# State's output behind the whole down projection, two PSUM banks exchanged, one addition of VectorE moved forward

## The chip, the cores and the metric

One core of a Trainium2 chip. The core has five engines that run side by side and wait for each other through semaphores: TensorE (PE: matmuls, reads SBUF, writes PSUM), VectorE (DVE), ScalarE (ACT), GpSimd (POOL, no access to PSUM) and SyncE (SP, which only issues transfers here). PSUM has eight banks of 128 x 512 fp32. The metric is the device time of one execution in microseconds; the median of the runs is given.

## What is computed

The input `x` has 8 sequences of 1024 tokens with 256 features. One block of a network, in fp32:

```
n  = layernorm(x)
xp, z = split(n @ w_in)                  # 512 features each
xc = silu(causal_conv(xp, 4 taps) + conv_b)
h_t = 0.9 * h_(t-1) + 0.1 * (xc_t @ w_B) # a state of 16 numbers, along the sequence
y  = (h @ w_C) * silu(z)
x  = x + y @ w_out
n  = layernorm(x)
idx = top2(n[:, token 0, :] @ Wr + br)   # two of eight experts for the whole sequence
x  = x + mean over idx of (gelu(n @ W1[e] + b1[e]) @ W2[e] + b2[e])
```

`h @ w_C` is "state's output", `xc @ w_B` "state's input", the last matmul the "down projection".

## The kernel before

**Tiles.** The 8192 tokens are cut into 16 chunks of 512 (two for a sequence; `NC` = 16, `LAST` = 15). Activations stand with features on the partitions and the 512 tokens along the free axis, so a block of 128 features is one PSUM bank. The 512 inner features are four blocks (`JD`), the hidden features of the two chosen experts four more (`JF`). Each fp32 operand is split into a high part (fp32r) and a low rest, and a product is three matmuls: high by high, high by low, low by high. Hence the many "hi" and "lo" tiles: ScalarE makes the high parts, VectorE or GpSimd the low ones.

**Steps.** The kernel is a software pipeline, written out by hand for each engine. Step s works on three chunks at once: the first half of the block on chunk a = s, the output projection of chunk o = s - 1, the experts of chunk f = s - 2. Steps 3 to 13 or so run through a loop that holds an even step (`q` = 0, in which the experts of a new sequence are chosen) and an odd one (`q` = 1); the first chunks are an opening of their own, and steps 15, 16 and 17 are written out.

**TensorE's order in a step** (`step`, L1571 to L1616), which is fixed: in an even step the six small score matmuls of the router; four blocks of the input projection (`xp`, 6 matmuls of 128x512 each) into banks blk0 to blk3; the output projection (`out_proj`, 48 matmuls of 128x256) into tok0 and tok1; four blocks of z; four blocks of the up projection (`up`), both into blk0 to blk3; state's input (`state_in`, 8 matmuls) into turn1; then the down projection (`down`, L1440), whose half 0 (tokens 0 to 255 of the chunk) goes to bank tok0 and half 1 to tok1, 24 matmuls of 128x256 a half, six for each hidden block. State's output (`state_out`, L1478, 4 matmuls of 128x512) stands in the middle of half 1: behind its hidden blocks 0 and 1 and in front of 2 and 3. Its four blocks go to blk0 to blk3, each behind the gelu that empties the bank. L1296, L1299 and L1305 are the three matmuls of `project`; L1419, L1420 and L1421 those of `tokens`, used by both the output and the down projection.

**What follows state's output.** VectorE multiplies each block by the gate (`ys`, L1048; semaphore `y_set` counts the blocks), ScalarE takes the high part (`y_his`, L737), GpSimd the low one (`split_y`, L485), and the output projection of the next step uses them. The bank of a block is free when the product is done, so block j of the next step's input projection waits for it (`xp`, L1324).

**VectorE's order at the end of a step** (L1146 to L1231): the low parts of the hidden blocks (`hidden_lo`), the scan over the 512 tokens (`scan`), `edge`, the low part of the state (`state_lo`), the low part of the next chunk's normalized block (`turn1_lo`), then the four products `ys`, then `finish(f, q, 0)` and `finish(f, q, 1)`. A `finish` (L1053) adds one half of the down projection (a PSUM bank tok) to the residual; it waits for `down_ready` of that half and for `b2_added`, GpSimd's addition of the bias (L498). Behind it stands the next step: in an even one the `route` (L1065, four tiny operations that read the score), then the convolution: three taps for each block on VectorE (L992), the first pair waiting for ScalarE's `first_taps` (L678), which reads the bank of the input projection.

**Banks.** turn1 holds state's input from chunk 2 on, read by the scan. turn0 holds the score of the middle pairs of chunks (`score_bank`, L249). In the last chunks both serve transposes.

**GpSimd's order in an even step** (L592 to L603): `split_y`, the reciprocal root and the norm of the next chunk (`pow1`, `norm1`), low parts of the chosen W1, two low parts of the convolution (`split_conv`), W2, the third, the statistics of the second norm, the fourth, the bias sum, the bias add. State's input waits for the low parts.

Of the kernel before, what the change touches and what calls it, by code (L numbers as in the profile page):

```python
# [22 lines left out]
def build_block(nc, x, w_in, conv_w, conv_b, w_B, w_C, w_out, Wr, br, W1, b1, W2, b2, out):  # L23
# [19 lines left out]
    with ExitStack() as ctx:  # L43
# [187 lines left out]
        def z_bank(a, j):  # L231
            if isinstance(a, int) and a < 3:
                return (tok[j % 2], spread_banks[j], (turn[1], tok[0], tok[1], tok[1])[j])[a]
            return blk[j]

        def c_bank(a, j):
            if isinstance(a, int) and a < 2:
                return (spread_banks[j], (blk[1], blk[2], tok[0], blk[3])[j])[a]
            return blk[j]

        def u_bank(a):
            if isinstance(a, int) and a < 2:
# [6 lines left out]
        def score_bank(pair):  # L249
            if isinstance(pair, int) and pair in (0, NC // 2 - 1):  # L250
                return blk[0] if pair else blk[1]
            return turn[0]

        def edges_before(c, pair):
            if isinstance(c, int) and c < 4:
# [15 lines left out]
        def has_attn(s):  # L271
            return not isinstance(s, int) or s <= LAST

        def has_next(s, ahead):
            return not isinstance(s, int) or s + ahead <= LAST
# [583 lines left out]
        def _(dve):  # L859
# [91 lines left out]
            def turn1_lo(c):  # L951
                for k in range(KD):
                    dve.wait_ge(t1_hi, c * KD + k + 1)
                    if on_pe(c):
                        lo(xn1(c)[1][:, k, :], turn[k][:], xn1(c)[0][:, k, :]).then_inc(t1_lo, 1)
                    else:
                        lo(in_order(xn1_lo, k), regrouped(normed1, k), in_order(xn1_hi, k)).then_inc(t1_lo, 1)
# [90 lines left out]
            def ys(a, js=range(JD)):  # L1048
                for j in js:
                    dve.wait_ge(c_ready, a * JD + j + 1)  # L1050
                    nc.vector.tensor_tensor(gate_of(a, j), c_bank(a, j)[:], gate_of(a, j), ALU.mult).then_inc(y_set, 1)

            def finish(f, q, h):  # L1053
                dve.wait_ge(down_ready, f * 2 + h + 1)
                dve.wait_ge(b2_added, f + 1)
                rows = mid(f, q)[:, half_rows(h), :].rearrange("p n d -> p (n d)")
                nc.vector.scalar_tensor_tensor(rows, tok[h][:], 1.0 / TOP_K, rows, ALU.mult, ALU.add).then_inc(done, 1)
# [88 lines left out]
            def step(s, q, half):  # L1146
                a, o, f = s, s - 1, s - 2
                halves = half - 1 if q == 0 else half
                if q == 0 and not has_attn(s):
                    last_split((1, 2, 3))  # L1150
                    route(half - 1)
                    finish(f - 1, 1, 1)
                    turn2_lo(f)
                    residual(o, 1, halves, 0)
                    residual(o, 1, halves, 1)
                    stats2(o, 1)
                    hidden_lo(f, range(JF))
                    norm2_last()
                    turn2_lo(o)
                    finish(f, 0, 0)  # L1160
                    finish(f, 0, 1)
                    return
                if q == 0:
                    route(half - 1)
                    if has_attn(s):
                        taps(a, 0)
                    turn_squares2(f)
                    if has_attn(s):
                        taps(a, 1)
                    residual(o, 1, halves, 0)  # L1170
                    residual(o, 1, halves, 1)
                    turn2_lo(f)
                    stats2(o, 1)
                    if has_next(s, 2):
                        stats1(a + 2)
                        moments1(a + 2)
                    if has_next(s, 1):
                        turn_squares(a + 1)
                    hidden_lo(f, range(JF))
                    if has_attn(s):  # L1180
                        scan(a, 0)
                    if has_next(s, 1):
                        edge(a + 1, False)
                    if has_attn(s):
                        state_lo(a, 0)
                    if has_next(s, 1):
                        turn1_lo(a + 1)
                    if has_attn(s):
                        ys(a)
                    finish(f, 0, 0)  # L1190
                    finish(f, 0, 1)
                    return
                if not has_attn(s):
                    hidden_lo(f, range(JF))
                    finish(f, 1, 0)
                    finish_tile(f, 1, 2, tok[1])
                    finish_tile(f, 1, 3, turn[0])
                    return
                taps(a, 0)
                if isinstance(a, int) and a == 3:  # L1200
                    taps(a, 1)
                    turn_squares2(f)
                    turn2_lo(f)
                else:
                    turn_squares2(f)
                    taps(a, 1)
                residual(o, 0, halves, 0)
                residual(o, 0, halves, 1)
                if not (isinstance(a, int) and a == 3):
                    turn2_lo(f)  # L1210
                stats2(o, 0)
                if has_next(s, 2):
                    stats1(a + 2)
                if has_next(s, 2):
                    moments1(a + 2)
                if has_next(s, 1):
                    turn_squares(a + 1)
                hidden_lo(f, range(JF))
                scan(a, 1)
                if has_next(s, 1):  # L1220
                    edge(a + 1, True)
                state_lo(a, 1)
                if has_next(s, 1):
                    turn1_lo(a + 1)
                if has_next(s, 1):
                    ys(a)
                    finish(f, 1, 0)
                    finish(f, 1, 1)
                else:
                    finish(f, 1, 0)  # L1230
                    ys(a)  # L1231

            opening()
            steps(dve, step)
# [2 lines left out]
        def _(pe):  # L1237
# [80 lines left out]
            def xp(a, j):  # L1318
                if isinstance(a, int) and a == 1:
                    pe.wait_ge(tap_added, last_tap(0, j))  # L1320
                elif isinstance(a, int) and a == 2:
                    pe.wait_ge(tap_added, last_tap(1, j))
                elif not (isinstance(a, int) and a == 0):
                    pe.wait_ge(y_set, a * JD - JD + j + 1)  # L1324
                in_proj(a, j, 0, blk[j], xp_ready)

            def xp_first():
# [243 lines left out]
            def step(s, q, half):  # L1571
                a, o, f = s, s - 1, s - 2
                if q == 0:
                    score(f, half - 1)
                if has_attn(s):
                    for j in range(JD):
                        xp(a, j)
                if has_out(s):
                    out_proj(o, 0, (x_tail, a + 1) if has_attn(s) else None)
                    out_proj(o, 1)  # L1580
                if has_attn(s):
                    z(a)
                if q == 0:
                    pe.wait_ge(route_step, half * 3 - 2)
                up(s, f, q, half - 1)
                if has_attn(s):
                    pe.wait_ge(t2_lo, f * KD + KD)
                    state_in(a)
                if q == 0 and has_attn(s):
                    pe.wait_ge(w2_lo_set, (half - 1) * TOP_K + TOP_K)  # L1590
                if has_out(s):
                    pe.wait_ge(mid_set, o * 2 + 2)
                else:
                    pe.wait_ge(done, f * 2 + 3)
                if not has_out(s):
                    down(f, 0, (0, 1, 2), (up_tail, 2))
                    pe.wait_ge(done, f * 2 + 4)
                    down_tile(f, 2, tok[1][:, 0:D], (0, 1, 2))
                    down(f, 0, (3,))
                    down_tile(f, 2, tok[1][:, 0:D], (3,))  # L1600
                    down_tile(f, 3, turn[0][:, 0:D])
                    return
                if isinstance(s, int) and s == NC:
                    down(f, 0, (0, 1, 2), (up_tail, 1))
                    down(f, 1, (0, 1))
                    down(f, 0, (3,))
                    turns2(o)
                    down(f, 1, (2, 3))
                    return
                down(f, 0, range(JF), (state_tail, a + 1))  # L1610
                down(f, 1, (0, 1))
                if has_attn(s):
                    state_out(a, s)
                if isinstance(s, int) and s == LAST:
                    turns2(LAST - 1)
                down(f, 1, (2, 3))  # L1616
# [27 lines left out]
```

## Time and profile before

| | us |
|---|---|
| median of 3 runs | 505.83 (505.81 to 506.48) |
| the profiled execution, whole | 507.02 |
| its span, from the first to the last instruction | 505.1 |
| busy: TensorE, VectorE, ScalarE, GpSimd | 500.6, 450.9, 401.3, 348.1 |

The time of an execution holds some two microseconds around the span. Busy time adds up the durations of an engine's instructions where they don't overlap. A matmul's recorded duration (about 0.39 us for 128x512, 0.28 for 128x256) is longer than the distance to the next one, because they are pipelined; how fast TensorE goes is read from the starts. A VectorE operation likewise may start a little before the recorded end of the one before.

### The profile page before, as it was taken

How to read it: one execution, taken by the hardware profiler on the slowest of the kernel's cores; microseconds unless marked ns; L12 is line 12 of the kernel's file. 1: busy time of each engine (PE TensorE's matmuls, PEld its weight loads, DVE VectorE, ACT ScalarE, POOL GpSimd, SP SyncE). 2: the span in 40 equal slices, each digit the busy share in tenths (PEclk: the TensorE clock that was granted, in tenths of full speed). 3: DMA queues.
4: the chain of work that ended last, by engine and by line, in shares of the span. 5: the costliest groups of instructions: out<-in, count | busy, mean ns of one | idle time of the engine just before them, and what ended most of it. 6: DMA issues, size and time to landing. Idle time of an engine off the chain costs nothing.

```text
span 505.1 us, 9943 instructions
## 1 busy us (share of the span) xinstructions
PE 500.6 (99%) x3026; PEld 442.7 (88%) x3026; DVE 450.9 (89%) x896; ACT 401.3 (79%) x692; POOL 348.1 (69%) x390
## 2 busy tenths in 40 slices
PE   8999999999999999999999999999999999999997
PEld 8888799888888988889888888988889889888997
DVE  6999999889998999989999899998999989996763
ACT  4986959888969788697987969878796888969454
POOL 4959597559693796929869197773977559673390
PEclk9999999999999999999999999999999999999999
DMA  8940105344250532605235170433614343130102
GB/s 254 300 180 7 37 1 183 110 135 160 77 191 27 166 125 86 204 30 193 68 126 165 48 227 16 166 125 100 191 42 150 99 132 120 59 108 1 42 3 84
DMA packets 53380, 57.29 MB, mean 113 GB/s; under 512 B 8682, under 2 KB 49642, under 8 KB 53226
## 3 DMA queue, kind: packets, MB, share of 16 engines
q1 hardware_dynamic: 51498, 56.67, 34.5%
q10 hardware_dynamic: 1856, 0.31, 0.3%
q8 instruction: 13, 0.21, 0.2%
q14 instruction: 13, 0.11, 0.1%
HBM read 35.46 MB, written 21.50 MB: 113 GB/s over the span
## 4 chain that ended last, share of the span: by engine, by line
PE 98%; DVE 1%; DMA 1%; issue 0%; DVEq 0%
PE blk L1296 16%; PE blk L1299 16%; PE blk L1305 16%; PE tok L1419 12%; PE tok L1420 12%; PE tok L1421 12%; PE blk L1494 3%; PE turn L1470 3%; PE turn L1473 3%; PE turn L1243 1%; PE tok L1299 1%; PE tok L1296 1%; PE tok L1305 1%; DMA x_mid<-in_L_attn_x 1%; DVE stats_t L917 0%; DVE normed L934 0%
## 5 line engine op out<-in xcount | busy, mean ns | idle before, releaser
L992 DVE SCALAR_TENSOR_TENSOR conv<-blk,tap_w,conv 128x512 f32<-128x512 f32 x192 | 130.1, 741 | 8.2 <-ACT conv L683 7.1
L488 POOL TENSOR_TENSOR y_lo<-gate,y_hi 128x512 fp32r<-128x512 f32 x57 | 72.2, 1297 | 35.5 <-ACT y_hi L611 35.4
L1296 PE MATMUL blk<-xn_hi,w_in_hi 128*128 128x512 f32 x228 | 89.4, 392 | 0.0
L1299 PE MATMUL blk<-xn_hi,w_in_lo 128*128 128x512 f32 x228 | 89.0, 391 | 0.0
L453 POOL TENSOR_TENSOR xc_lo<-conv,xc_hi 128x512 fp32r<-128x512 f32 x60 | 72.9, 1232 | 7.9 <-ACT xc_hi L611 7.7
L1419 PE MATMUL tok<-w_out_hi,y_hi 128*128 128x256 f32 x256 | 71.7, 280 | 0.0
L1420 PE MATMUL tok<-w_out_lo,y_hi 128*128 128x256 f32 x256 | 71.1, 278 | 0.0
L1421 PE MATMUL tok<-w_out_hi,y_lo 128*128 128x256 f32 x256 | 71.1, 278 | 0.0
L1305 PE MATMUL blk<-xn_lo,w_in_hi 128*128 128x512 f32 x228 | 70.3, 390 | 0.0
L1419 PE MATMUL tok<-w_hi,hid_hi 128*128 128x256 f32 x248 | 70.0, 282 | 0.0
L1421 PE MATMUL tok<-w_hi,hid_lo 128*128 128x256 f32 x248 | 69.6, 281 | 0.0
L1420 PE MATMUL tok<-w_lo,hid_hi 128*128 128x256 f32 x248 | 69.6, 281 | 0.0
L683 ACT ACTIVATE conv<-blk,tap_b,tap_w 128x512 f32<-128x512 f32 x64 | 49.3, 781 | 25.4 <-PE blk L1305 22.2
L689 ACT ACTIVATE conv<-conv 128x512 f32<-128x512 f32 x64 | 39.4, 632 | 30.3 <-DVE conv L992 29.4
L861 DVE TENSOR_TENSOR hid_lo<-hid,hid_hi 128x512 fp32r<-128x512 f32 x64 | 44.8, 728 | 17.1 <-ACT hid_hi L611 16.9
L498 POOL TENSOR_TENSOR x_mid<-x_mid,b_sel 128x256 f32<-128x256 f32 x60 | 45.7, 792 | 13.5 <-DVE hid_lo L861 9.4
L1305 PEld LDWEIGHTS blk<-xn_lo,w_in_hi 128*128 128x128 f32 x228 | 42.8, 188 | 9.1
L1419 PEld LDWEIGHTS tok<-w_out_hi,y_hi 128*128 128x128 f32 x256 | 48.3, 189 | 2.7 <-issue 2.6
L1299 PEld LDWEIGHTS blk<-xn_hi,w_in_lo 128*128 128x128 f32 x228 | 42.9, 188 | 8.1
L1419 PEld LDWEIGHTS tok<-w_hi,hid_hi 128*128 128x128 f32 x248 | 47.1, 190 | 3.1 <-issue 2.6
L1296 PEld LDWEIGHTS blk<-xn_hi,w_in_hi 128*128 128x128 f32 x228 | 42.8, 188 | 8.0
L1296 PE MATMUL blk<-xn_hi,w_hi 128*128 128x512 f32 x124 | 48.4, 390 | 0.0
(189 smaller groups left out, 1320.5 us busy)
## 6 DMA issues: line engine op xcount, KB each, us to landing
spill<-normed SPq DMA_DIRECT2D x25, 512.0 KB, 2.8
normed<-spill SPq DMA_DIRECT2D x100, 128.0 KB, 2.8
out<-x_mid SPq DMA_DIRECT2D x30, 256.0 KB, 2.5
x_mid<-in_L_attn_x SPq DMA_DIRECT2D x29, 256.0 KB, 2.7
x_in<-in_L_attn_x SPq DMA_DIRECT2D x14, 512.0 KB, 4.3
w_all<-in_L_ffn_W SPq DMA_DIRECT2D x2, 2048.0 KB, 11.4
b_all<-in_L_ffn_b SPq DMA_DIRECT2D x1, 1024.0 KB, 13.6
gate<-in_L_attn_w_in SPq DMA_DIRECT2D x2, 256.0 KB, 4.5
```

Of the source, the lines that this page charges most:

```text
L453: nc.gpsimd.tensor_tensor(xc_lo[:, j, :], conv[:, j, 0:CH], xc_hi[:, j, :].bitcast(F32), ALU.subtract).then_inc(xc_lo_set, 1)
L488: nc.gpsimd.tensor_tensor(y_lo[:, j, :], gate_of(o, j), y_hi[:, j, :].bitcast(F32), ALU.subtract).then_inc(y_lo_set, 1)
L498: ins = nc.gpsimd.tensor_tensor(mid(f, q)[:, n, :], mid(f, q)[:, n, :], b2_sel[:], ALU.add)
L683: nc.scalar.activation(conv[:, j, HALO:HALO + CH], blk[j][:], ACT.Identity, bias=tap_b[:, j:j + 1], scale=tap_w[:, j, 0:1]).then_inc(tap_f ...
L861: return nc.vector.tensor_tensor(dst, src, hi.bitcast(F32), ALU.subtract)
L992: nc.vector.scalar_tensor_tensor(cols, blk[j][:], tap_w[:, j, t:t + 1], cols, ALU.mult, ALU.add).then_inc(tap_added, 1)
L1296: ins = mm(dst, whi(k), his(k), start=(k == 0), stop=False)
L1299: mm(dst, wlo(k), his(k), start=False, stop=False)
L1305: ins = mm(dst, whi(k), los(k), start=False, stop=(k == KD - 1))
L1419: mm(dst, his[:, j, rows], whi, start=(j == 0 and n == 0), stop=False, skip_group_check=True)
L1420: mm(dst, his[:, j, rows], wlo, start=False, stop=False, skip_group_check=True)
L1421: ins = mm(dst, los[:, j, rows], whi, start=False, stop=(last and n == 1), skip_group_check=True)
```

## The change

It has four parts. (1) In steps 3 to 14 state's output stands behind the whole of down projection half 1. (2) Its block 0 goes to bank turn0 there, and the score moves from turn0 to turn1. (3) Block 0 of the next input projection therefore waits no longer for `y_set` but for the gelu that read its bank. (4) VectorE does `finish(f, q, 0)` in front of the products in all steps that have them in the loop's form. Step 15 keeps its order on every engine.

```diff
+        def state_last(a):
+            return not isinstance(a, int) or 3 <= a < LAST
+
         def c_bank(a, j):
             if isinstance(a, int) and a < 2:
                 return (spread_banks[j], (blk[1], blk[2], tok[0], blk[3])[j])[a]
-            return blk[j]
+            return turn[0] if state_last(a) and j == 0 else blk[j]
...
         def score_bank(pair):
             if isinstance(pair, int) and pair in (0, NC // 2 - 1):
                 return blk[0] if pair else blk[1]
-            return turn[0]
+            return turn[1]
...
                     if has_next(s, 1):
                         turn1_lo(a + 1)
+                    finish(f, 0, 0)
                     if has_attn(s):
                         ys(a)
-                    finish(f, 0, 0)
                     finish(f, 0, 1)
                     return
...
                 if has_next(s, 1):
                     turn1_lo(a + 1)
+                finish(f, 1, 0)
+                ys(a)
                 if has_next(s, 1):
-                    ys(a)
-                    finish(f, 1, 0)
                     finish(f, 1, 1)
-                else:
-                    finish(f, 1, 0)
-                    ys(a)
...
                 elif not (isinstance(a, int) and a == 0):
-                    pe.wait_ge(y_set, a * JD - JD + j + 1)
+                    if j == 0 and state_last(a - 1):
+                        pe.wait_ge(gelu_set, (a - 3) * JF + 1)
+                    else:
+                        pe.wait_ge(y_set, a * JD - JD + j + 1)
                 in_proj(a, j, 0, blk[j], xp_ready)
...
                 down(f, 0, range(JF), (state_tail, a + 1))
+                if state_last(a):
+                    down(f, 1)
+                    state_out(a, s)
+                    return
                 down(f, 1, (0, 1))
                 if has_attn(s):
                     state_out(a, s)
```

## Rows read from the trace of the kernel before

**Rows 1.** The page: busy time by engine, busy tenths and clock in 40 slices.
```profile
PE 500.6 (99%) x3026; PEld 442.7 (88%) x3026; DVE 450.9 (89%) x896; ACT 401.3 (79%) x692; POOL 348.1 (69%) x390
...
PEclk9999999999999999999999999999999999999999
```

**Rows 2.** The waits of TensorE, whole run: us in total, times, longest.
```profile
PE tok L1523 <- POOL ident L397: 1.6, 1, 1.6
PE turn L1252 <- DVE normed L934: 0.2, 1, 0.2
```

**Rows 3.** Timeline of TensorE, state's input of step 10: start, duration, engine, line.
```profile
311.74 1.07 PE L1470 MATMUL turn<-xc_hi,b_mix 128*128 128x512 f32 x4
312.65 1.07 PE L1473 MATMUL turn<-xc_lo,b_mix 128*128 128x512 f32 x4
```

**Rows 4.** Timeline of TensorE, state's output of steps 9 and 10, next input projection.
```profile
287.32 1.09 PE L1494 MATMUL blk<-state_mix,c_mix 128*128 128x512 f32 x4
...
317.80 1.09 PE L1494 MATMUL blk<-state_mix,c_mix 128*128 128x512 f32 x4
318.73 0.28 PE L1419 MATMUL tok<-w_hi,hid_hi 128*128 128x256 f32 x1
...
320.14 0.40 PE L1296 MATMUL blk<-xn_hi,w_in_hi 128*128 128x512 f32 x1
...
321.07 0.62 PE L1305 MATMUL blk<-xn_lo,w_in_hi 128*128 128x512 f32 x2
```

**Rows 5.** Timeline of TensorE, end of an output projection, next z.
```profile
238.72 0.28 PE L1419 MATMUL tok<-w_out_hi,y_hi 128*128 128x256 f32 x1
...
240.08 0.40 PE L1296 MATMUL blk<-xn_hi,w_in_hi 128*128 128x512 f32 x1
```

**Rows 6.** Timeline of ScalarE, step 10: gelu 0, splits of the products, first taps.
```profile
308.52 0.67 ACT L728 ACTIVATE hid<-blk,b_sel 128x512 f32<-128x512 f32 x1
...
319.91 2.43 ACT L611 ACTIVATE y_hi<-gate 128x512 fp32r<-128x512 f32 x4 [0.87 <-DVE gate L1051]
322.24 1.63 ACT L683 ACTIVATE conv<-blk,tap_b,tap_w 128x512 f32<-128x512 f32 x2
```

**Rows 7.** Timeline of VectorE, the products of step 10.
```profile
319.20 2.47 DVE L1051 TENSOR_TENSOR gate<-blk,gate 128x512 f32<-128x512 f32 x4
```

**Rows 8.** Timeline of TensorE's weight loads, blocks 0 and 1 of input projection 11.
```profile
320.03 0.19 PEld L1296 LDWEIGHTS blk<-xn_hi,w_in_hi 128*128 128x128 f32 x1
...
321.31 0.19 PEld L1296 LDWEIGHTS blk<-xn_hi,w_in_hi 128*128 128x128 f32 x1
```

**Rows 9.** Timeline of GpSimd, step 10: gated output, fourth low part, bias add.
```profile
289.19 5.05 POOL L488 TENSOR_TENSOR y_lo<-gate,y_hi 128x512 fp32r<-128x512 f32 x4 [1.02 <-ACT y_hi L611]
...
309.74 1.29 POOL L453 TENSOR_TENSOR xc_lo<-conv,xc_hi 128x512 fp32r<-128x512 f32 x1
...
314.85 3.28 POOL L498 TENSOR_TENSOR x_mid<-x_mid,b_sel 128x256 f32<-128x256 f32 x4 [2.06 <-DVE hid_lo L861]
```

**Rows 10.** Timeline of VectorE, end of step 9 and first taps of step 10.
```profile
287.75 2.48 DVE L1051 TENSOR_TENSOR gate<-blk,gate 128x512 f32<-128x512 f32 x4
...
291.35 0.14 DVE L1068 TENSOR_TENSOR scores<-turn,b_router 1x8 f32<-1x8 f32 x1
...
292.30 0.75 DVE L992 SCALAR_TENSOR_TENSOR conv<-blk,tap_w,conv 128x512 f32<-128x512 f32 x1
293.67 3.39 DVE L992 SCALAR_TENSOR_TENSOR conv<-blk,tap_w,conv 128x512 f32<-128x512 f32 x5 [0.61 <-ACT conv L683]
```

**Rows 11.** Timeline of ScalarE, the first first-tap of step 10.
```profile
291.49 0.78 ACT L683 ACTIVATE conv<-blk,tap_b,tap_w 128x512 f32<-128x512 f32 x1 [0.58 <-PE blk L1305]
```

**Rows 12.** Timeline of TensorE, start of step 10's output projection.
```profile
295.37 0.29 PE L1419 MATMUL tok<-w_out_hi,y_hi 128*128 128x256 f32 x1
```

**Rows 13.** Timeline of SyncE, the spill of the normalized block.
```profile
297.62 0.35 SPq L326 DMA_DIRECT2D spill<-normed  x1
```

**Rows 14.** Busy time by engine between two state's outputs: span, then busy (instructions).
```profile
317.80:348.04 30.24, 30.24 (x182) 26.73 (x181) 27.79 (x55) 24.93 (x42) 17.71 (x20) 1.00 0.34 106
```

## The prediction

> **What bounds the kernel now.** I read the page's engine table first [rows 1]: TensorE is busy 500.6 of 505.1 us, VectorE 450.9, and the granted clock stands in its highest tenth in every slice, so the clock is not at stake. Busy TensorE rows prove little by themselves, because their ends overlap; so the next view is its waits [rows 2]. It waits twice in the whole run, 1.8 us in sum, both before the loop. The third reading is spacing: inside a run of equal matmuls, does each start when it should? Four 128x512 matmuls in mid-run take 311.74 to 312.65 [rows 3], 0.227 us each. In the stretch that the change touches, twelve 128x256 matmuls take 318.73 to 320.14, 0.1175 us each, and nothing stands between them and their neighbours [rows 4]. So TensorE has no hole at state's output, and none at the first input block behind it. Whatever VectorE gains there, TensorE can't start sooner.
>
> Step 10 (state's output at 317.80) stands for the even steps, step 9 (287.32) for the odd ones [rows 4]; the change acts in steps 3 to 14, twelve in all. The others look alike within 0.1 us, except 4 and 14, which have 0.2 to 0.5 us more room on VectorE, and step 3.
>
> **TensorE's order.** The same matmuls run; only the twelve of the last two hidden blocks and the four of state's output swap places. Their work is 1.41 us and 0.93 us in either order. One thing can shrink. A run of 128x512 matmuls that follows 128x256 ones starts slower: the first four take 0.93 us, both in state's output (317.80 to 318.73) and in the input projection (320.14 to 321.07) [rows 4], against 0.91 in mid-run [rows 3]. Before, each step enters such a run twice here; afterwards state's output leads straight into the input projection of the next step, with only the tiny score between in every second one. That saves 0.02 to 0.03 us a step, in 12 steps 0.2 to 0.35; I take 0.3. Bounds: nothing if the slow start belongs to the operands and not to the order; a gain of 0.9 if beside it the twelve moved matmuls ran at the output projection's 0.113 (238.72 to 240.08 is twelve in 1.36 [rows 5]), which is 0.05 us a step more; a loss of 0.6 if they slowed by as much. I take the entry alone, since the moved matmuls keep their operands and are nearest to their own rows.
>
> The Trainium skill (TensorE: Matmul & The Clock Gate, Back-to-back issue gap) gives a matmul's spacing by its columns alone. By that rule an order costs nothing, the gain is 0 and the time stays 505.8. The rows differ from it by the 0.02 us at an entry.
>
> **The waits of the input projection.** Block 0 no longer waits for VectorE's product but for the gelu that emptied its bank: in step 10 that ended at 308.52 + 0.67 = 309.19 [rows 6], 11 us earlier, so the new wait is free. What goes was free too: the first product ended at 319.20 + 0.68 = 319.88 [rows 7], and the weights of block 0 load at 320.03 [rows 8]; 0.15 us of room was enough. Blocks 1 to 3 still wait for their products, and those now come later.
>
> **VectorE in an even step.** It gets to the products late, at 319.20 [rows 7], though their first bank was full at 317.80 + 0.39. Now a half add stands first. Four products take 2.47 us and the last lasts 0.68, so operations start 0.60 apart. State's output now begins at 317.80 + 1.41 = 319.21 and its first bank is full at 319.60. Half add at 319.20, first product at 319.80, second at 320.40, done 321.08. The weights of block 1 load at 321.31 [rows 8]: 0.2 us of room, as much as block 0 had. Blocks 2 and 3 gain 0.7 us of room each, as a block takes 1.36 and a product 0.60. The second half add ends as before: no idle, no loss. Its bias is there: GpSimd's adds end at 314.85 + 3.28 = 318.13 [rows 9], 1.1 us before. Behind the products, ScalarE's splits begin 0.6 later (319.91 before), and so does its first tap (322.24 before [rows 6]); it waits 0.58 for a later block [rows 11], which takes that in.
>
> **VectorE in an odd step.** Here it is on time: products from 287.75, half adds behind, the route at 291.35 [rows 10]. Now: half add at 287.75, done 288.43; state's output starts at 287.32 + 1.41 = 288.73, its first bank is full at 289.12, and VectorE starts 0.04 later (as 287.71 to 287.75 before): 0.75 us idle. Products at 289.16, 289.76, 290.36, 290.96, the second half add at 291.56, the route at 292.16: 0.8 late. The route and its waits take 0.95, so the first tap stands at 293.1. Before it started at 292.30, and the second waited 0.61 for ScalarE until 293.67 [rows 10]. ScalarE's splits now run 289.88 to 292.3 and its first taps start at 292.3 and 293.0 (291.49 the first before [rows 11]), so the second tap starts at 293.75: of 0.8 us some 0.1 is left. That 0.1 travels through step 10, where VectorE has hardly any idle before the products, and lowers the room of 0.2 to 0.1. In the odd step itself block 1 has 0.6 of room (product done at 290.44, weights at about 291.1).
>
> **GpSimd.** Its split of the gated output starts at 289.19 and takes 5.05 for four blocks [rows 9]; with the products 1.4 later it starts at 290.6, has block 0 at 291.9 and block 3 at 295.7. The output projection begins at 295.37 [rows 12] and reaches block 3 some 2.0 later. The chain behind has no idle until the bias add: everything moves by 1.4. What TensorE needs of it last is the fourth low half, done at 309.74 + 1.29 = 311.03 [rows 9], now 312.4; TensorE takes it as the fourth of the group at 312.65 [rows 3], whose weights load at about 313.1. Room 0.7. The bias add waited 2.06 for VectorE [rows 9] and takes 1.4 in. In even steps GpSimd moves by 0.6 only.
>
> **SyncE and the banks.** The first half's store may go sooner, the second's 0.8 later in an odd step. SyncE's queue keeps its order: stores, refills, then the spill of the normalized block, which waits for GpSimd and moves from 297.62 [rows 13] by 1.4; VectorE takes the regrouped block late in the step, behind all its statistics. The score writes another bank, whose last reader, the scan, stands before the products: free. The last step (15) and the tail keep their order.
>
> **The sum.** -0.3 for the entries, 0 for every wait. The profiled execution took 507.02 us (span 505.1) and would take 506.7; the median of the runs is 505.83, 1.2 below it, so I forecast 505.5. A measurement of this kernel can tell about 0.2% (1.0 us) from no change, so this is "same".
>
> **Rivals.**
> A, nothing at all: TensorE is as full in the new order and the entry keeps its cost, 505.8. The gapless rows speak for it; so the change would then do what it says, where nobody waited.
> B, slower: block 1 of the input projection waits for the second product in even steps. It decides once VectorE is over 0.1 us later there than I reckoned. Against it: the second tap's old wait of 0.61 swallows the delay. For it: the room is that small, and the waiting matmul holds back all behind it. With the full 0.8 carried, the product ends at 321.88, 0.57 after the weights' turn: four steps of 0.57 and 0.45 in 4 and 14 together, 2.7 in all: 508.2. With half of it, 0.17 in four steps: 506.2.
> The skill has a rule that leans this way (VectorE: DVE Perf Modes, The DRAIN you can't avoid): an operation starts only when the one before has left the pipe. By it operations would stand 0.68 apart and the second product, with the 0.1, end 0.03 too late: 505.6. The rows show 0.60 apart instead.
> C, slower through GpSimd: its chain moves by over 2.1 us and state's input waits for the low half. Reckoned is 1.4; at 2.5 it is 0.4 in six steps, 507.9.
> D, faster: all 48 hidden-block matmuls of a step are slow (0.1175 against 0.113) because of what else runs, and the new order frees them. 0.2 us in twelve steps, 2.4, and the entry: 503.1; a third of it is 504.7. Against it: the 30.24 us from step 10's state output to step 11's [rows 14] are 84 matmuls of 0.227, 48 of 0.1175 and 48 of 0.113, 30.1, whatever stood beside them; nothing else is left to save.
>
> **How the numbers follow.** Forecast 0.53, A 0.27, B 0.09 (0.03 of it within the bound), C 0.02, D 0.09 (0.03 within). Within 0.2%: 0.53 + 0.27 + 0.03 + 0.03 = 0.86; faster 0.06, slower 0.08. The range goes from 504.9, the moved matmuls quickened, to 506.6, which holds A with the spread of the runs (505.81 to 506.48) and the mild form of B.
>
> **What would show it.** State's output runs straight into the input projection, whose first four take 0.91. VectorE idles 0.7 to 0.8 before the products in odd steps and not in even ones; a half add stands before them. The second tap's wait for ScalarE shrinks from 0.6 to near 0.1. TensorE's waits stay at two; that stretch stays at 30.2. I am wrong if TensorE's waits name the gated product or the low half, or if the spacing inside equal matmuls changes.

## The result: slower by 1.2%

The changed kernel takes 512.03 us (median of 4 runs, 511.41 to 513.15); the kernel before 505.9. The ratio is 1.0121, with an interval of 1.0102 to 1.014: 6.1 us lost. The forecast was 505.5, within 504.9 to 506.6.

The page of the changed kernel, engine by engine [rows 1], then TensorE's waits [rows 2]:

```profile
PE 501.1 (98%) x3026; PEld 440.9 (86%) x3026; DVE 463.4 (91%) x896; ACT 397.9 (78%) x692; POOL 350.1 (68%) x390
...
PEclk9999999999999999999999999999999999999999
```
```profile
PE tok L1422 <- DVE hid_lo L864: 5.5, 5, 1.2
PE tok L1526 <- POOL ident L400: 1.6, 1, 1.6
PE turn L1252 <- DVE normed L937: 0.3, 1, 0.3
```

The clock is the same and TensorE's work is the same. It has a new wait, five times about 1.1 us, at the first matmul of the down projection, for the first hidden low part of VectorE. And VectorE, with the same 896 instructions, is busy 12.5 us longer: its operations have grown, and only some of them. Over the whole run the 50 low parts `xn_lo` take 9.7 us more (45.2 before, 54.9 now) and the 16 `var_eps` of the second norm 6.7 more (2.5, 9.2), while `neg_mean` gives back 1.9 (in odd steps the pair of low parts grows too, from 1.7 to 2.8 us, and TensorE doesn't wait for it); taps, statistics and products keep theirs within 1 us. (In the changed file the lines from the tap on are 3 higher: L861 is now L864, L1419 is L1422.)

The step table by state's inputs tells where: from the even step 10's to step 11's took 30.24 us before (311.74 to 341.98) and 31.38 now (315.31 to 346.69); the odd step in front 30.48 before and 30.52 now. Twelve such steps add 6.4 us, of which the five even steps 4 to 12 hold 6.0. By stretches, the twelve are 6.7 longer from state's input to the down projection, 0.2 in the input projection, and 0.4 and 0.2 shorter in the down and the output projection.

TensorE in step 10, where the hole is, and at state's output [rows 3, 4]:

```profile
316.21 1.07 PE L1476 MATMUL turn<-xc_lo,b_mix 128*128 128x512 f32 x4
318.35 0.36 PE L1422 MATMUL tok<-w_hi,hid_hi 128*128 128x256 f32 x1 [1.06 <-DVE hid_lo L864]
...
323.89 0.40 PE L1497 MATMUL turn<-state_mix,c_mix 128*128 128x512 f32 x1
324.12 0.86 PE L1497 MATMUL blk<-state_mix,c_mix 128*128 128x512 f32 x3
324.82 0.39 PE L1296 MATMUL blk<-xn_hi,w_in_hi 128*128 128x512 f32 x1
...
325.73 0.39 PE L1305 MATMUL blk<-xn_lo,w_in_hi 128*128 128x512 f32 x1
```

Four matmuls of state's input used to end in a down projection 0.91 us behind their start; now it is 2.14. State's output runs into the input projection, whose first four take 0.91 (324.82 to 325.73): the forecast's saving of 0.02 is there. It is there in even steps only. In odd ones, where the score stands between, the input projection takes 5.55 us before and after. And it is not all that moved. In step 10 the 48 matmuls of the down projection take 5.54 (318.35 to 323.89) and not the 5.66 of before (4.24 and 1.41 on either side of state's output): behind the hole they go over from 0.118 us each to 0.113 after the first few.

**VectorE, odd step.** The end of step 9 [rows 10]:

```profile
291.49 0.68 DVE L1060 SCALAR_TENSOR_TENSOR x_mid<-tok,x_mid 128x512 f32<-128x512 f32 x1
292.69 0.69 DVE L1054 TENSOR_TENSOR gate<-turn,gate 128x512 f32<-128x512 f32 x1 [0.52 <-PE turn L1497]
293.30 1.87 DVE L1054 TENSOR_TENSOR gate<-blk,gate 128x512 f32<-128x512 f32 x3
...
295.69 0.14 DVE L1071 TENSOR_TENSOR scores<-turn,b_router 1x8 f32<-1x8 f32 x1
```

From the half add's start to the route 4.20 us: reckoned were 287.75 to 292.16, 4.41. The half add starts 0.2 later than reckoned and the idle time behind it is 0.52 instead of 0.75, so against TensorE the route is 0.8 late, as reckoned. The taps then take the delay in: measured from step 9's state input, the first taps and the transpose behind them end 0.03 us later than before. Up to here the forecast holds.

**VectorE, even step.** Behind the taps it does not. First the kernel before, then the changed one, from the low parts of the second norm on. The rows of before were not among those on which the forecast rested:

```profile
303.35 2.68 DVE L861 TENSOR_TENSOR xn_lo<-normed,xn_hi 128x512 fp32r<-128x512 f32 x2
...
307.91 0.34 DVE L911 TENSOR_SCALAR neg_mean<-mean_var 128x4 f32<-128x4 f32 x1
308.17 0.16 DVE L912 TENSOR_SCALAR var_eps<-mean_var 128x4 f32<-128x4 f32 x1
```
```profile
306.90 3.26 DVE L864 TENSOR_TENSOR xn_lo<-normed,xn_hi 128x512 fp32r<-128x512 f32 x2
...
312.05 0.17 DVE L914 TENSOR_SCALAR neg_mean<-mean_var 128x4 f32<-128x4 f32 x1
312.13 1.07 DVE L915 TENSOR_SCALAR var_eps<-mean_var 128x4 f32<-128x4 f32 x1
```

The pair of low parts takes 0.58 more, and an operation on 128x4 numbers 1.07 instead of 0.16. GpSimd at the same times, before and after:

```profile
304.41 1.08 POOL L471 CAST w_hi<-w_all 128x512 fp32r x1
305.68 1.51 POOL L474 TENSOR_TENSOR w_lo<-w_all,w_hi 128x512 fp32r<-128x512 f32 x1 [0.19 <-POOL w_hi L471]
307.14 1.08 POOL L453 TENSOR_TENSOR xc_lo<-conv,xc_hi 128x512 fp32r<-128x512 f32 x1
```
```profile
308.11 1.51 POOL L477 TENSOR_TENSOR w_lo<-w_all,w_hi 128x512 fp32r<-128x512 f32 x1 [0.19 <-POOL w_hi L474]
...
312.07 1.10 POOL L456 TENSOR_TENSOR xc_lo<-conv,xc_hi 128x512 fp32r<-128x512 f32 x1
```

Read the ends. The small operation ends at 312.13 + 1.07 = 313.20, GpSimd's running one at 312.07 + 1.10 = 313.17. The pair of low parts ends at 310.16, which is 0.54 behind the end of GpSimd's W2 low part (309.62); before it ended at 306.03, 0.54 behind the end of a cast (305.49). Before, `neg_mean` took 0.34 and ended (308.25) just behind GpSimd's 308.22, so the small one behind it met a gap. So the idea: some VectorE operations can't finish while a GpSimd instruction is in flight; GpSimd's chain now comes 1.4 us later, against a VectorE that stands where it stood, and each meets another neighbour. That makes VectorE 1.3 us late for the hidden low parts (312.20 is 0.46 behind state's input before, 317.08 is 1.77 now).

### The profile page after: what moved, and what is told of

Its sections match the earlier page's. It is cut to its first block, busy times and chain, and to the rows that moved or that the text cites. A ratio compares the mean times of both kernels' runs of the same rounds, so it can differ in the third digit from the quotient of the medians.

```text
span 511.3 us, 9938 instructions
## 1 busy us (share of the span) xinstructions
PE 501.1 (98%) x3026; PEld 440.9 (86%) x3026; DVE 463.4 (91%) x896; ACT 397.9 (78%) x692; POOL 350.1 (68%) x390
## 4 chain that ended last, share of the span: by engine, by line
PE 73%; DVE 12%; issue 10%; ACT 3%; DMA 1%; DVEq 0%; ACTq 0%
PE blk L1296 10%; PE blk L1299 10%; PE blk L1305 10%; PE tok L1422 10%; PE tok L1423 10%; PE tok L1424 10%; DVE conv L995 3%; ACT y_hi L614 2%; DVE xn_lo L864 2%; PE turn L1473 2%; PE turn L1476 2%; PE blk L1497 1%; DVE stats_t L875 1%; DVE stats_t L901 1%; DVE normed L978 1%
## 5 line engine op out<-in xcount | busy, mean ns | idle before, releaser
L456 POOL TENSOR_TENSOR xc_lo<-conv,xc_hi 128x512 fp32r<-128x512 f32 x60 | 74.0, 1252 | 5.9 <-ACT xc_hi L614 5.8
L1422 PE MATMUL tok<-w_hi,hid_hi 128*128 128x256 f32 x248 | 70.1, 283 | 5.6 <-DVE hid_lo L864 5.5
L1422 PE MATMUL tok<-w_out_hi,y_hi 128*128 128x256 f32 x256 | 71.6, 280 | 0.0
L1424 PE MATMUL tok<-w_out_hi,y_lo 128*128 128x256 f32 x256 | 71.0, 277 | 0.0
L1424 PE MATMUL tok<-w_hi,hid_lo 128*128 128x256 f32 x248 | 69.3, 279 | 0.0
L686 ACT ACTIVATE conv<-blk,tap_b,tap_w 128x512 f32<-128x512 f32 x64 | 47.8, 776 | 14.3 <-PE blk L1305 11.5
L864 DVE TENSOR_TENSOR xn_lo<-normed,xn_hi 128x512 fp32r<-128x512 f32 x50 | 54.9, 1137 | 1.4 <-ACT xn_hi L614 0.7
L1422 PEld LDWEIGHTS tok<-w_hi,hid_hi 128*128 128x128 f32 x248 | 47.0, 190 | 9.6 <-issue 9.6
L864 DVE TENSOR_TENSOR hid_lo<-hid,hid_hi 128x512 fp32r<-128x512 f32 x64 | 43.6, 718 | 10.0 <-ACT hid_hi L614 9.7
L614 ACT ACTIVATE y_hi<-gate 128x512 fp32r<-128x512 f32 x60 | 36.2, 633 | 20.3 <-DVE gate L1054 20.3
L1422 PEld LDWEIGHTS tok<-w_out_hi,y_hi 128*128 128x128 f32 x256 | 48.3, 188 | 2.8 <-issue 2.6
```

What stands on the lines that cost most here:

```text
L456: nc.gpsimd.tensor_tensor(xc_lo[:, j, :], conv[:, j, 0:CH], xc_hi[:, j, :].bitcast(F32), ALU.subtract).then_inc(xc_lo_set, 1)
L614: return nc.scalar.activation(dst, src, ACT.Copy, scale=scale)
L686: nc.scalar.activation(conv[:, j, HALO:HALO + CH], blk[j][:], ACT.Identity, bias=tap_b[:, j:j + 1], scale=tap_w[:, j, 0:1]).then_inc(tap_f ...
L864: return nc.vector.tensor_tensor(dst, src, hi.bitcast(F32), ALU.subtract)
L1422: mm(dst, his[:, j, rows], whi, start=(j == 0 and n == 0), stop=False, skip_group_check=True)
L1424: ins = mm(dst, los[:, j, rows], whi, start=False, stop=(last and n == 1), skip_group_check=True)
```

## The experiments

**Theory 1** is the idea above: the delay of the products in odd steps moves GpSimd; GpSimd's new phase stretches VectorE in even steps; TensorE waits. **Theory 2**: the even step's own new order (late state's output, half add first) does it. A third, in e3: VectorE's own delay of 0.8 us is enough, and GpSimd has no part. Ratios are against the kernel before, on the same chip (its median went from 506.1 to 507.6 over the chips).

**e1, the change in even steps only; e2, in odd steps only.** The edit, with 0 for e1 and 1 for e2 (VectorE's order in the other kind of step is the old one; the score is in turn1 in both):

```diff
         def state_last(a, behind=0):
-            return not isinstance(a, int) or 3 <= a < LAST
+            q = a % 2 if isinstance(a, int) else (now[0] + behind) % 2
+            return (not isinstance(a, int) or 3 <= a < LAST) and q == 0
```

> The change in even steps only (state's output behind the down projection, block 0 in turn0, half add first); odd steps keep the old order, the score stays in turn1. Theory 1: the loss comes through GpSimd, whose chain of an even step starts 1.4 us later because the products of the odd step in front are 1.4 later; VectorE's operations then meet other GpSimd instructions and grow by 1.36 us. Here the odd step keeps its time, so GpSimd keeps its phase: no wait of TensorE for the hidden low part, 505.5 to 506.2. Theory 2: state's output or the half add of the even step itself is what hurts: 511 to 512 as with the whole change.

> The change in odd steps only. Theory 1: GpSimd's chain in the next even step starts 1.4 us later, TensorE waits about 1.1 us at the down projection of each of five even steps: 510.5 to 512. Theory 2 (the even step's own order): 505.5 to 506.5.

e1: ratio 1.0005 (0.9995 to 1.0015), no difference. (Its trace isn't quite the old one: ahead of the down projections of steps 3 to 14 it loses 1.2 us, 0.4 of it named as waits for the hidden low part, and its 128x256 matmuls give back 1.0.) e2: 1.0125 (1.0107 to 1.0143), the whole loss, with the same wait and the same stretched operation:

```profile
PE tok L1427 <- DVE hid_lo L869: 5.6, 5, 1.1
```
```profile
307.53 3.28 DVE L869 TENSOR_TENSOR xn_lo<-normed,xn_hi 128x512 fp32r<-128x512 f32 x2
...
312.77 1.07 DVE L920 TENSOR_SCALAR var_eps<-mean_var 128x4 f32<-128x4 f32 x1
```

The harm appears in even steps and is made in odd ones. Theory 2 falls.

**e3 and e5, GpSimd alone later.** TensorE, VectorE and the banks as before:

```diff
                 if has_attn(s):
                     split_y(o)
+                    if q == 0:
+                        nc.gpsimd.tensor_tensor(filler[:, 0:4], decay[:, 0:4], minus_half[:], ALU.pow)
+                        nc.gpsimd.memset(filler[:, 8:], 0.0)
```

> The kernel before, with a power of 4 values (about 1.0 us) and a memset of 512 (about 0.45 us) put on GpSimd behind its split of the gated output in even steps; TensorE, VectorE and the banks as before. Theory 1: GpSimd's chain is 1.4 us late and VectorE's low part of the second norm (2.68 us for two) and a statistics operation (0.16 us) grow as after the change, to 3.26 and 1.07; TensorE waits for the hidden low part: 509.5 to 512. Rival: VectorE's lateness comes from its own order (route 0.8 us later), and GpSimd's has no part in it: 505.6 to 506.2, as GpSimd alone had 0.7 us or more of room to every wait of TensorE.

e3: 1.0204 (1.0187 to 1.0221), more than theory 1 gives. The pair takes 3.28, the small operation 1.07, TensorE waits for the hidden low part in five steps; but besides, the output projection takes 5.65 us (332.52 to 338.17) instead of 5.47, and 5.64 to 5.71 in every step of the loop. The scratch tile stood ahead of y and hid and had moved them. e5 puts it last:

> The same delay of GpSimd as in e3_gp_later (power of 4 and memset of 512 behind its split of the gated output, even steps), but its scratch tile stands last in SBUF, so that no other tile moves. In e3_gp_later the tile stood ahead of y and hid, and the output projection's 48 matmuls took 5.65 us a step instead of 5.47. Theory 1 with placement as the second cause: output projection back at 5.47, TensorE's waits for the hidden low part as in e3, 510.5 to 512.5. If the slower output projection came from the delay itself: 516 again.

```profile
PE tok L1423 <- DVE hid_lo L865: 6.1, 5, 1.6
```
```profile
307.64 3.35 DVE L865 TENSOR_TENSOR xn_lo<-normed,xn_hi 128x512 fp32r<-128x512 f32 x2
...
312.96 1.07 DVE L916 TENSOR_SCALAR var_eps<-mean_var 128x4 f32<-128x4 f32 x1
```

The output projection is back at 5.47 (331.28 to 336.75). Ratio 1.014 (1.0123 to 1.0157), 7.1 us. The profiled run took 513.36, the median 514.63, above the 512.5 that I gave; its chip was the one where the kernel before took 507.62. A delay on GpSimd alone, with nothing of the change, makes the loss, so GpSimd has a part. Whether VectorE's own delay would be enough without GpSimd's is not settled here, but in e7.

**e6, the tile alone**, at the place of e3 and without an instruction (`filler = sb("filler", [P, 8 + 512])` behind `behind_columns`):

> The kernel before with the scratch tile of e3_gp_later allocated at the same place (y and hid move by 2080 bytes) and no instruction added. If the placement of the stationary tiles sets the spacing of the 128x256 matmuls: output projection 5.65 us a step (0.118 for one) instead of 5.47, 16 steps, 508 to 509.5. Else 505.8 to 506.5.

1.006 (1.0043 to 1.0077), 3.0 us. The output projection:

```profile
327.92 0.28 PE L1420 MATMUL tok<-w_out_hi,y_hi 128*128 128x256 f32 x1
...
333.61 0.40 PE L1297 MATMUL blk<-xn_hi,w_in_hi 128*128 128x512 f32 x1
```

5.69 us, and 5.67 to 5.71 in steps 3 to 14. So e3 was two effects, and placement is a cause of its own.

**e4, the half add alone; e12, TensorE's order alone.** e4 is the kernel before with `finish(f, q, 0)` ahead of `ys(a)`; e12 the changed kernel with `ys(a)` ahead of both.

> The kernel before with VectorE's half add in front of the products, TensorE and the banks as before. The products are 0.6 us later in both kinds of step, so GpSimd's chain of an even step is 0.6 late and not 1.4. Theory 1: other meetings, not necessarily worse ones; between 505 and 509, with TensorE's only new wait at the down projection or at block 0 of the input projection, whose product now ends 0.45 us after the turn of its weights in even steps (about 0.4 us in each of six steps, 508.3). Rival (GpSimd without a part): 508.3 from that wait at block 0 alone.

> The changed TensorE order and banks with VectorE's old order (four products, then both half adds): the other half of e4_half_first. Theory 1: in an odd step the products start when state's output allows, 1.37 us later than before, so GpSimd's chain of the even step is as late as with the whole change, the statistics operation takes 1.07 and TensorE waits about 1.1 us at the down projection of five even steps: 510.5 to 512.5. If the loss needed the half add in front of the products: 505.5 to 507.

e12: 1.0107 (1.009 to 1.0124), with waits of 5.4 us for the hidden low part. e4: 1.0104 (1.0087 to 1.0121), which is more than I had given any theory. TensorE's waits in e4:

```profile
PE blk L1293 <- DVE gate L1051: 2.0, 5, 0.5
...
PE tok L1416 <- DVE hid_lo L861: 1.6, 5, 0.6
PE blk L1249 <- DVE normed L934: 0.6, 1, 0.6
PE turn L1249 <- DVE normed L934: 0.5, 1, 0.5
```
```profile
311.05 1.07 DVE L912 TENSOR_SCALAR var_eps<-mean_var 128x4 f32<-128x4 f32 x1
```

A delay of 0.6 us of the odd step's products is enough for the small operation to meet GpSimd (the pair takes 2.40 there, less than before), and TensorE waits 1.6 us for the hidden low part. The larger wait, 2.0, is another thing: the product of block 0 comes too late for the next input projection, as expected. The last two rows stand in the tail of the kernel. So either half of the change costs about what the whole does, but not in the same way. In e12 all of TensorE's new wait is for the hidden low part: VectorE is itself 0.5 late at the pair (it starts 7.84 us ahead of step 10's state input, 8.39 before), and the small operation adds 0.9. In e4 the hidden low part has less than half of it.

**e7, GpSimd sooner in the changed kernel.** `choose_w1` makes the second expert's low part for 16 of 512 columns in the loop, and so leaves out most of that part of the result (`w1_lo[:, t, 0:n]`, n = 16 for t = 1).

> The changed kernel, GpSimd's chain of the even steps shortened by about 1.1 us: the low part of the second expert's W1 is made for 16 of 512 columns only, from the second sequence on (the rest keeps the values of the first). Theory 1: GpSimd's later instructions are back near the places of the kernel before, VectorE's statistics operation takes 0.16 again, the low parts of the second norm less than 3.26: most of the 1.1 us of wait at the down projection goes, 506 to 508. Rival (VectorE's lateness has another source in the change): 511 to 512.5.

1.0021 (1.0011 to 1.0031): the median is 508.65 (506.22 to 509.16) beside 507.62.

```profile
PE tok L1424 <- DVE hid_lo L866: 1.2, 5, 0.3
```
```profile
303.39 2.40 DVE L866 TENSOR_TENSOR xn_lo<-normed,xn_hi 128x512 fp32r<-128x512 f32 x2
...
307.75 1.07 DVE L917 TENSOR_SCALAR var_eps<-mean_var 128x4 f32<-128x4 f32 x1
```

With the change in full, VectorE's own delay with it, and GpSimd a good microsecond sooner, four fifths of the loss go by the medians. So that delay alone isn't enough, and the third theory falls. The profiled run is the fastest of the eleven, 2.4 us under their median, so its waits are a better witness than its time. From state's input to the down projection an even step takes 2.21 (step 10) where it took 1.81 before and 3.04 after the change: two thirds of the hole are gone. The rest of the run's speed is in the matmuls: its down projections take 5.47 in odd steps instead of 5.66. Not as I had it in detail: the small operation still takes 1.07, and the gain comes from the pair (2.40 instead of 3.26).

**e8, the hidden low parts first** (a mend of the whole change):

```diff
+                    hidden_lo(f, range(JF))
                     if has_next(s, 1):
                         turn_squares(a + 1)
-                    hidden_lo(f, range(JF))
```

> The changed kernel with VectorE's four hidden low parts moved ahead of the squares' transpose (1.16 us) of the next chunk in even steps. VectorE meets GpSimd as badly as before, but the first hidden low part is done 1.16 us sooner, and scan, state and products keep their time. If TensorE's wait at the down projection is the whole loss: 505.3 to 506.8, no wait there. If the lateness costs elsewhere too (products, taps): 508 to 511.

1.0101 (1.0084 to 1.0118): it mends nearly nothing. VectorE and GpSimd:

```profile
315.59 3.24 DVE L864 TENSOR_TENSOR hid_lo<-hid,hid_hi 128x512 fp32r<-128x512 f32 x4
```
```profile
315.54 0.73 POOL L483 TENSOR_TENSOR b_sum<-b_all 128x256 f32 x1
316.48 1.06 POOL L486 TENSOR_SCALAR b_sel<-b_sum 128x256 f32<-128x256 f32 x1 [0.20 <-POOL b_sum L483]
```

Moved ahead, the four low parts meet GpSimd's bias sum and take 3.24 instead of 2.48: the first ends at 316.82, 0.55 behind GpSimd's 316.27. TensorE still waits 0.5 there, and then for the product of block 1 (0.8 in three steps): it arrives 0.56 sooner than in the changed kernel, while the products stand where they stood, 9.4 us behind state's input. My expectation that nothing would happen but a shift repeated the mistake of the forecast.

**e11, the meeting by itself**, behind the last step of the kernel before. VectorE's series is a 128x4 `tensor_scalar`, `bn_stats`, `tensor_scalar`, a product with one input in PSUM, a difference of two SBUF tiles; twice beside GpSimd's differences of two tiles, once beside its memsets.

> The kernel before with a probe behind its last step: twice VectorE runs 128x4 tensor_scalar, bn_stats, 128x4 tensor_scalar, a product with one input in PSUM, a difference of two SBUF tiles, while GpSimd runs six differences of 128x512 (about 1.3 us each), then once while GpSimd only runs memsets. Theory 1 (VectorE waits for a GpSimd instruction in flight when it needs what they share): in the first part the difference of two SBUF tiles takes up to 1.9 us instead of 0.69 and some tensor_scalar up to 1.4 instead of 0.16, each ending just behind the end of a GpSimd row, while bn_stats (0.41) and the product with PSUM (0.68) keep theirs; beside memsets the difference of two tiles keeps 0.69. Rival (the growth in the loop is a wait for a semaphore or a slower memory): durations as alone in all parts, or all kinds grow alike. About 8 us longer in all.

```profile
503.48 1.27 DVE L1250 TENSOR_SCALAR unit<-minus_half 128x4 f32<-128x4 f32 x1
504.67 0.41 DVE L1251 BATCH_NORM_STATS2 stats_t<-normed 128x6 f32<-128x256 f32 x1
505.01 0.97 DVE L1252 TENSOR_SCALAR unit<-minus_half 128x4 f32<-128x4 f32 x1
505.89 0.68 DVE L1254 TENSOR_TENSOR normed<-blk,gate 128x512 f32<-128x512 f32 x1
506.49 1.23 DVE L1255 TENSOR_TENSOR xn_lo<-hid,gate 128x512 fp32r<-128x512 f32 x1
...
512.22 1.89 DVE L1254 TENSOR_TENSOR normed<-blk,gate 128x512 f32<-128x512 f32 x1
512.83 1.29 DVE L1255 TENSOR_TENSOR xn_lo<-hid,gate 128x512 fp32r<-128x512 f32 x1
```
```profile
503.47 5.37 POOL L611 TENSOR_TENSOR y_lo<-gate,hid 128x512 fp32r<-128x512 f32 x4 [9.29 <-DVEq L1258]
508.80 2.48 POOL L613 TENSOR_TENSOR xc_lo<-gate,hid 128x512 fp32r<-128x512 f32 x2
```

Beside GpSimd's differences the 128x4 operation takes 1.27 and 0.97 instead of 0.16, and the difference of two tiles 1.23 instead of 0.69; `bn_stats` (0.41) and the product with PSUM (0.68) keep their time. GpSimd's instructions, taken one by one, end at 504.73, 505.95, 507.17 and 508.84: the two small operations end 0.03 us behind one of them (504.76, 505.98), the difference 0.55 behind one (507.72). It goes the other way too: GpSimd's fourth difference, which starts during VectorE's, takes 1.71 us instead of 1.26. Two kinds are stopped, two are not, as theory 1 has it. The last two rows stand beside memsets; all five of that series are shown ending together at 514.10 to 514.11, so their durations can't be read and I take nothing from that part.

**e9 and e10, other places for the hidden tiles** (64 and 128 unused bytes ahead of `hid_hi`):

> The kernel before with 64 unused bytes ahead of the stationary tiles of the down projection (hid_hi, hid_lo), nothing else. In e6_tiles_moved a shift of y and hid by 2080 bytes (32 modulo 64) slowed the output projection's matmuls from 0.114 to 0.118 us each. If the down projection's 0.118 is a matter of the distance between the stationary and the moving tile, another distance (here 64 bytes more) may bring 0.113: 48 matmuls in each of 16 steps, 3 us less, 502.5 to 503.5. If not: 505.8 to 506.5, or up to 509 where it gets worse.

> As e9_hid_64 with 128 bytes. Same alternatives: 502.5 to 503.5, or 505.8 to 506.5.

e9: 1.0041 (1.0028 to 1.0054), slower. e10: 1.0008 (0.9998 to 1.0018), no difference, though the 36 matmuls of the down projection ahead of state's output take 4.10 us in step 10 instead of 4.24:

```profile
313.52 0.29 PE L1420 MATMUL tok<-w_hi,hid_hi 128*128 128x256 f32 x1
...
317.62 0.43 PE L1495 MATMUL blk<-state_mix,c_mix 128*128 128x512 f32 x1
```

Step 10 gains 0.03 of it in all. Step 4 gives 0.5 back (30.75 instead of 30.24), 0.4 of it ahead of its down projection, and step 11 0.25, in an output projection of 5.69 instead of 5.47. Nor is it shown that the place made the 4.10: in the traces of e1, e4 and e5, where `hid` stands where it stood before, the same 36 matmuls take 4.11 in most odd steps. No version beat the kernel before; e1, the change in even steps, costs nothing and gains nothing.

## Why the prediction was wrong

Point by point.

**What bounds the kernel, and that this order gains nothing**: right. TensorE was gapless before the change, and e1 with half of it is at 1.0005.

**TensorE's order**: right in sign, too large in size. The forecast took the entry's 0.02 to 0.03 us in all twelve steps, 0.3 in sum. It shows in even steps only, 0.02 or 0.03 in six of them, too small to be measured.

**The spacing of the matmuls**: the forecast kept it fixed, and gave as a sign of being wrong that it changes. It did. Rival D had said that the hidden matmuls are slow because of what else runs; the forecast answered that the step adds up "whatever stood beside them". With the same tiles at the same places the 48 take 5.53 or 5.54 us in steps 4, 8, 10 and 14 of the changed kernel, 5.73 in 6 and 12, and 5.66 in odd ones. In e7 and e12 the odd ones take 5.47 with no wait in front. This one is from e12, first matmul and the one behind the last:

```profile
347.34 0.28 PE L1425 MATMUL tok<-w_hi,hid_hi 128*128 128x256 f32 x1
...
352.81 0.40 PE L1500 MATMUL turn<-state_mix,c_mix 128*128 128x512 f32 x1
```

So D was right that something else sets the spacing, and wrong in that the new order frees it: the changed kernel got back 0.4 us in all of its down projections. What sets it is open.

**The new wait of block 0, the even step's products**: right but for one step. Rival B, to which I gave 0.09, came once: in step 14 the weights of block 1 wait 0.4 us for the gated product, and this is most of what that step lost. (e4 waits for block 0, 2.0 us; e8 for block 1, 0.8.)

**VectorE in the odd step**: right as to its end. Route 0.8 later, the taps take it in; the idle time in the middle was 0.52 and not 0.75.

**"That 0.1 travels through step 10, where VectorE has hardly any idle before the products"**: this is the step that failed. It took VectorE's durations as fixed, while the next paragraph moved GpSimd by 1.4 us underneath it. "Everything moves by 1.4" was right (GpSimd's third convolution low part starts 1.40 later, measured from step 9's state input), and so was its room to TensorE's waits: rival C, GpSimd's own low half too late for TensorE, didn't come. The delay came through the durations of VectorE: 0.58 on the pair, 0.9 on the small operation, 1.3 in all at the hidden low parts. The views held the sign of it: a 128x4 operation (`neg_mean`, L885) took 0.17 us in odd steps and 0.86 in even ones, and the same pair of low parts 2.68 in step 10 and 1.73 in step 9.

The Trainium skill states the rule (SBUF — State Buffer, Who interferes with whom): VectorE and GpSimd share one pair of ports as an exclusive lock. An operation with two SBUF inputs contends with a GpSimd instruction that reads SBUF, and so does one in a two-port mode, which a `tensor_scalar` can enter; there whoever issues first has the pair for the whole instruction. An operation with at most one SBUF input outside these modes doesn't contend. Probe and traces agree: 1.27 and 1.23 beside GpSimd, 0.68 and 0.41 for the kinds that the rule exempts, and 1.71 for the GpSimd instruction that came second. That rule would have made the durations of VectorE at GpSimd's new phase a rival of its own, and I had none.

**The wait that the forecast left out.** It weighed two waits of TensorE, the product and the convolution's low part, and not the one for the first hidden low part. That one had no room at all. TensorE's weight loads at the start of the down projection, before and after:

```profile
313.46 0.19 PEld L1419 LDWEIGHTS tok<-w_hi,hid_hi 128*128 128x128 f32 x1 [0.16 <-issue]
```
```profile
318.31 0.19 PEld L1422 LDWEIGHTS tok<-w_hi,hid_hi 128*128 128x128 f32 x1 [1.46 <-issue]
```

The low part ended at 312.20 + 0.67 = 312.87 before and at 317.08 + 0.67 = 317.75 after: the load follows 0.59 and 0.56 later. In e7, e8 and e12 it is 0.57 each time. A semaphore increment, a second wait and three more increments (`behind`, L1424) stand between the wait and the first matmul; that they are what the 0.57 consists of was not tried. By the wait rows the low part seemed to have 0.6 us of room; with these 0.57 it had about none, and VectorE's 1.3 us went through to TensorE almost whole: the five steps are 1.1 to 1.3 longer.

**Sizes.** 6.0 us in steps 4 to 12 is the ratio's 6.1. Step 14, with more room on VectorE, lost 0.3 (30.43 to 30.70), most of it at block 1.

## What to carry to other kernels

Where one engine is moved against another and both work on SBUF, don't add up old durations: list the VectorE operations with two SBUF inputs or a small `tensor_scalar`, lay GpSimd's instructions beside them at their new times, and let each wait for the end of what it meets, and GpSimd's for VectorE's. Look for one operation that has two durations in the same trace; that is the sign. And before a delay is called absorbed, take every wait of the bounding engine in the step, and measure its room to the first instruction behind the wait, not to the wait itself.

## What the runs showed of the hardware

- A VectorE operation with two SBUF inputs ends 0.54 to 0.55 us behind the end of the GpSimd instruction that it met (306.03 behind 305.49, 310.16 behind 309.62, 316.82 behind 316.27, in the probe 507.72 behind 507.17); a 128x4 `tensor_scalar` 0.03 behind (313.20 and 313.17).
- A delay of 0.6 us on VectorE's products is enough for the small operation to take 1.07 us instead of 0.16, as one of 1.4 us does. The hidden low parts come 0.5 us later there and 1.3 here, since the pair takes 2.40 in the one case and 3.26 in the other: the loss is made of meetings, each of which is there or not.
- The spacing of 128x256 matmuls is mostly at one of two values, 0.113 to 0.114 and 0.118 to 0.119 us. The place of the stationary tiles has a part: y and hid 2080 bytes further on took the output projection from 5.47 to 5.69 us a step and the kernel up by 0.6%. It isn't the only one: with the tiles where they were, the down projection of odd steps takes 5.66 after the change and 5.47 in e12, and the output projection of the kernel before 5.47 in most steps and 5.66 in two of the last. What chooses there stays open.
